# Last inverses of the first attention repeated on TensorE instead of through device memory, one-product gate bias, and a norm that lags two tiles

## The reference

```
xn = layernorm(x)
# layer 0, attention: 16 heads, two softmax maps per head, 32 output columns per head
a1, a2 = softmax(q1 k1' / 4 + causal), softmax(q2 k2' / 4 + causal)
lam    = exp(sum(lambda_q1*lambda_k1)) - exp(sum(lambda_q2*lambda_k2)) + 0.2
out    = (a1 - lam * a2) @ v                       # [T, 512]
out    = groupnorm over (time, 32 columns) of each head, times gn_w plus gn_b
s      = (0.8 * out) @ Wo
# layer 0, gate
g      = silu(mxfp4(xn) @ mxfp4(weight).T + bias)
x      = x + s * g
xn     = layernorm(x)                              # input of layer 1: attention and experts
```

## Time and profile before

| | |
|---|---|
| median of 3 runs | 843.96 us (841.63, 843.96, 844.77) |
| profiled execution | 842.62 us, of which the span of the trace is 840.9 us |
| PE busy | 775.1 us, 92% of the span |
| DVE / ACT / POOL busy | 530.1 / 429.3 / 425.7 us |
| granted TensorE clock, slices of 21 us | full, except 0.5 in the slice 378 to 399 us and 0.8 in the one after |
| middle block | 375.5 to 466.6 us |

### The profile page before, as it was taken

How to read it: one execution, slowest core, us unless ns; L and a number is a source line. 1 busy time by engine, 2 the same in 40 slices (tenths; PEclk the granted TensorE clock), 3 DMA queues, 4 the chain that set the end, 5 groups by cost and what they waited for, 6 DMA issues and landing times. The chain is left out here.

```text
span 840.9 us, 13145 instructions
## 1 busy us (share of the span) xinstructions
PE 775.1 (92%) x3822; PEld 376.3 (45%) x3826; DVE 530.1 (63%) x1352; ACT 429.3 (51%) x922; POOL 425.7 (51%) x754
## 2 busy tenths in 40 slices
PE   2988999999999999985889899999889999999995
PEld 2353222222222222221655323333167888888883
DVE  3657887778777777603562688787066654555556
ACT  2431466666666666661223157777744454455552
POOL 1661465664224324422232122334378997799994
PEclk9999999999999999995899999999999999999997
DMA  6391751020011002012019445235332221112221
GB/s 188 115 291 65 177 117 30 20 61 15 21 41 39 21 18 63 15 39 82 0 67 240 149 108 140 92 108 181 97 106 66 67 62 60 49 64 62 62 66 57
DMA packets 57960, 69.84 MB, mean 83 GB/s; under 512 B 13813, under 2 KB 35670, under 8 KB 57895
## 3 DMA queue, kind: packets, MB, share of 16 engines
q1 hardware_dynamic: 57820, 69.08, 29.2%
q10 hardware_dynamic: 80, 0.07, 0.0%
HBM read 47.35 MB, written 15.47 MB: 75 GB/s over the span
## 5 line engine op out<-in xcount | busy, mean ns | idle before, releaser
L763 ACT ACTIVATE top<-ps 128x512 f32<-128x512 f32 (+3 forms) x384 | 170.6, 491 | 132.5 <-PE ps L691 132.5
L691 PE MATMUL ps<-mid 99*128 99x512 bf16 (+3 forms) x576 | 182.5, 332 | 4.2 <-ACT mid L763 3.1
L808 DVE CUSTOM_DVE_ANT_0 ps<-ps,keep 128x512 f32<-128x512 f32 (+3 forms) x320 | 161.8, 530 | 30.3 <-PE ps L667 30.2
L667 PE MATMUL ps<-mid 96*128 96x512 bf16 (+3 forms) x512 | 167.1, 339 | 4.6 <-DVE mid L808 1.0
L711 PE MATMUL ps<-top,mid 128*33 128x512 f32 (+3 forms) x768 | 161.7, 500 | 0.0
L1559 PE MATMUL ps<-xp,wp 128*128 128x512 f32 (+1 forms) x600 | 146.8, 394 | 5.4 <-ACT wp L1609 3.6
L691 PEld LDWEIGHTS ps<-mid 99*128 99x128 bf16 x576 | 53.5, 97 | 173.0 <-ACT top L763 103.3
L1559 PEld LDWEIGHTS ps<-xp,wp 128*128 128x128 f32 (+1 forms) x600 | 112.4, 188 | 31.9 <-ACT xp L1611 4.1
L900 POOL TENSOR_SCALAR_AFFINE_SELECT top<-top 128x128 f32<-128x128 f32 x256 | 71.2, 292 | 106.1 <-ACT top L763 104.1
L763 ACT ACTIVATE mid<-ps 128x512 f32<-128x512 f32 (+1 forms) x192 | 82.1, 494 | 63.3 <-PE ps L691 40.6
L812 DVE TENSOR_REDUCE top<-ps 128x1 f32<-128x512 f32 x128 | 88.3, 690 | 33.0 <-PE ps L667 32.8
(11 more groups left out here) (208 smaller groups left out, 887.0 us busy)
## 6 DMA issues: line engine op xcount, KB each, us to landing
mid<-part_scratch SPq DMA_DIRECT2D x9, 1152.0 KB, 8.8
part_scratch<-top SPq DMA_DIRECT2D x18, 384.0 KB, 5.1
top<-in_w SPq DMA_DIRECT2D x12, 528.0 KB, 4.7
cw_s<-combine_rows SPq DMA_DIRECT2D x48, 128.0 KB, 3.0
part_scratch<-top SPq DMA_DIRECT2D x18, 256.0 KB, 5.1
mid<-part_scratch SPq DMA_DIRECT2D x9, 384.0 KB, 4.2
top<-inverse_scratch SPq DMA_DIRECT2D x12, 256.0 KB
top<-in_w SPq DMA_DIRECT2D x6, 512.0 KB, 6.5
```

Of the source, the lines that this page charges most:

```text
L667: nc.tensor.matmul(ps[:, s_bank(turn), 0:w], queries(pair, m)[0:PARTS, i * P:(i + 1) * P], keys(pair, m)[0:PARTS, c * 512:c * 512 + w], st ...
L691: nc.tensor.matmul(ps[:, ST_BANK + n % AHEAD, 0:w], keys(pair, m)[0:STACK, j * P:(j + 1) * P], queries(pair, m)[0:STACK, q0:q0 + w], start ...
L763: nc.scalar.activation(pr[:, n % RING, 0:w], ps[:, ST_BANK + n % AHEAD, 0:w], ACT.Exp, scale=0.25).then_inc(p_ready, 1)
L808: ins = nc.vector.tensor_tensor_reduce(bank, bank, msk[:, 512 - w:512], -1.0 if low else 1.0, 3e38 if low else -3e38, ALU.add, ALU.min if ...
```

## The change

In words, in the order of the program:

- **Bias.** The bias is loaded on 65 partitions (it was one). DVE splits it in three bf16 parts on all of them and puts them in the rows 0, 32 and 64 of a `bip` of 65 rows that is zero elsewhere. `row` has 65 rows of ones. `ffn(t)` then has one bias product in place of three.
- **Last inverses.** For the last heads of the first attention alone, `inverses` is replaced by `inverse_rows`: one DMA from `cd[:, c, 0, :]` (128x32) to eight rows of 512 in SBUF, `repeated(c)[0][0:8, :]`. PE repeats them (`repeat_rows`): two fp32 products of 8x128 against 8x512, with a 0/1 matrix `heads` that POOL writes at the start of the block from the identity. c = 0 goes to the banks 6 and 7 ahead of all else on PE; c = 1 to the banks 2 and 3 behind ffn(1). ffn(4) waits until c = 0 has been read (`row_stats` 7).
- **Division.** `divide` on DVE does what POOL's `scale` and DVE's `combine` did: map 1 times lambda times its bank, map 0 times its bank, the sum, and `bn_stats`. It stands first on DVE for c = 0, and behind gate2(1) for c = 1. POOL has no division left in the middle block. gate2(2) and gate2(3) move behind the scaling. SP no longer waits for the inverses before it loads the next weights.
- **Norm two behind.** DVE does `norm2(t-2)` in tile t, PE the transposes of t-3 and the logits of t-4, and the first two projections one step later in the loop, which has one turn more.

```diff
-        bip = sb("bip", [1, 3, D], BF16, keep)
+        bip = sb("bip", [65, D], BF16, keep)
...
-                    sp.dma_start(bia[:, :], fb).then_inc(ld_r, 16)
+                    sp.dma_start(bia[:, :], fb.partition_broadcast(65)).then_inc(ld_r, 16)
...
-                    link(nc.vector.tensor_copy(bip[:, 0, :], bia[:, :]))
-                    link(nc.vector.tensor_tensor(bir[:, :], bia[:, :], bip[:, 0, :], ALU.subtract))
-                    link(nc.vector.tensor_copy(bip[:, 1, :], bir[:, :]))
-                    link(nc.vector.tensor_tensor(bip[:, 2, :], bir[:, :], bip[:, 1, :], ALU.subtract))
+                    link(nc.vector.memset(bip[:, :], 0.0))
+                    link(nc.vector.tensor_copy(bih[:, :], bia[:, :]))
+                    nc.vector.tensor_copy(bip[0:1, :], bih[0:1, :])
+                    link(nc.vector.tensor_tensor(bir[:, :], bia[:, :], bih[:, :], ALU.subtract))
+                    link(nc.vector.tensor_copy(bim[:, :], bir[:, :]))
+                    nc.vector.tensor_copy(bip[32:33, :], bim[32:33, :])
+                    link(nc.vector.tensor_tensor(bip[64:65, :], bir[64:65, :], bim[64:65, :], ALU.subtract))
...
+            def inverse_rows(sp, c):
+
+                sp.wait_ge(inv, 2 * LASTF + c + 1)
+                sp.wait_ge(scaled, 2 * (LASTF - 1) + c + 1)
+                sp.dma_start(repeated(c)[0][0:8, :], cd[:, c, 0, :]).then_inc(inv_r[c], 16)
+
+            def repeat_rows(pe, c, heads, banks):
+
+                pe.wait_ge(inv_r[c], READS * LASTF + 16)
+                for m, bank in enumerate(banks):
+                    last = nc.tensor.matmul(ps[:, bank, :], heads[:, m, :], repeated(c)[0][0:8, :], start=True, stop=True)
+                return last
+
+            def divide(dve, c, banks):
+
+                to, n1 = o1[:, LASTF, columns(c)], second(LASTF)[:, c, :]
+                nc.vector.scalar_tensor_tensor(n1, n1, lamv[:, 1:2], ps[:, banks[1], :], ALU.mult, ALU.mult).then_inc(scaled, 1)
+                dve.wait_ge(scaled, 2 * LASTF + c + 1)
+                nc.vector.tensor_tensor(to, to, ps[:, banks[0], :], ALU.mult).then_inc(combined, 1)
+                dve.wait_ge(combined, 2 * (LASTF + c) + 1)
+                nc.vector.tensor_tensor(to, to, n1, ALU.add).then_inc(combined, 1)
+                dve.wait_ge(combined, 2 * (LASTF + c) + 2)
+                nc.vector.bn_stats(st6o[:, LASTF, c, :], to).then_inc(row_stats, 1)
...
-                env["last_inverses0"](sp)
+                env["inverse_rows"](sp, 1)
...
+                for m in range(2):
+                    nc.gpsimd.tensor_copy(heads[:, m, :].rearrange("p (h d) -> p h d", h=4),
+                                          idf[0:8, m:8:2].unsqueeze(2).to_broadcast([8, 4, 32])).then_inc(bip_ok, 1)
                 nc.gpsimd.memset(row[:, :], 1.0).then_inc(bip_ok, 1)
-                env["last_scaled0"](pool)
...
+                dve.wait_ge(tot, 1)
+                env["divide"](dve, 0, (6, 7))
                 env["last_inverted0"](dve)
...
-                env["last_combined0"](dve, 0)
-                for t in range(4):
+                for t in range(2):
                     gate2(t)
-                link(env["last_scaled_odd0"](dve))
-                env["last_combined0"](dve, 1)
+                dve.wait_ge(tot, 2)
+                env["divide"](dve, 1, (2, 3))
...
-                    if t >= 1:
-                        norm2(dve, t - 1)
+                    if t >= 2:
+                        norm2(dve, t - 2)
...
+                pe.wait_ge(bip_ok, 3)
+                env["repeat_rows"](pe, 0, heads, (6, 7)).then_inc(tot, 1)
...
-                    for j in range(3):
-                        last = nc.tensor.matmul(z, row[:, :], bip[:, j, :], start=False, stop=j == 2)
-                    last.then_inc(f_mm, 1)
+                    nc.tensor.matmul(z, row[:, :], bip[:, :], start=False, stop=True).then_inc(f_mm, 1)
...
                 for t in range(NT):
+                    if t == 4:
+                        pe.wait_ge(row_stats, 7)
                     ffn(t)
+                    if t == 1:
+                        env["repeat_rows"](pe, 1, heads, (2, 3)).then_inc(tot, 1)
                     if t >= 6:
                         total(t - 6)
```

More of the change, by code:

```diff
@@ L225, in program @@
             le = sb("le", [P, 2], F32)
-            bia, bir = (sb(n, [1, D], F32) for n in ("bia", "bir"))
+            bia, bir = (sb(n, [65, D], F32) for n in ("bia", "bir"))
+            bih, bim = (sb(n, [65, D], BF16, keep) for n in ("bih", "bim"))
             ld_x, ld_w, ld_c, ld_f, ld_r = (sem(n, a) for n in ("ld_x", "ld_w", "ld_c", "ld_f", "ld_r"))
@@ L524, in last_inverses @@
                 inverses(sp, LASTF, 1)
[L525 to L526 removed]
+            def inverse_rows(sp, c):
[16 more added lines that the diff above has]
+                nc.vector.bn_stats(st6o[:, LASTF, c, :], to).then_inc(row_stats, 1)
             def last_inverted(dve):
                 inverted(dve, LASTF, 1)
[L531 to L532 removed]
             def last_scaled(eng):
                 scale(eng, LASTF, 0)
[L536 to L541 removed]
+                scale(eng, LASTF, 1)
             with ExitStack() as b:
@@ L978, in _ @@
                             sp.dma_start(w2s[0:NI - (GI - 1) * P, GI - 1, :], w2[(GI - 1) * P:NI, :]).then_inc(ld_m, 16)
-                        inverses(sp, LASTF, 0)
+                        if first:
+                            inverse_rows(sp, 0)
+                        else:
+                            inverses(sp, LASTF, 0)
                         sp.wait_ge(landed, 32 * (N + 1))
             here[1] = kept
-            return o1, combined, last_inverses, last_inverted, last_scaled, last_combined, last_outputs, last_scaled_odd
+            if first:
+                return last_outputs, last_inverted, inverse_rows, repeat_rows, divide
+            return o1, combined, last_outputs, last_inverted, last_inverses, last_scaled
         tmp[1] = 0
@@ L1002, in late0 @@
                 far_maps0(sp, pair + 1)
-        o0, combined0, last_inverses0, last_inverted0, last_scaled0, last_combined0, last_outputs0, last_scaled_odd0 = attention(
+        last_outputs0, last_inverted0, inverse_rows, repeat_rows, divide = attention(
             0, stack0, v0, 16, loaded0, late0)
@@ L1040, in late1 @@
                 far_maps1(sp, (3, 1)[pair])
-        o1, combined1, last_inverses, last_inverted, last_scaled, _, last_outputs, _ = attention(
+        o1, combined1, last_outputs, last_inverted, last_inverses, last_scaled = attention(
             1, stack1, v1, 8, loaded1, late1)
@@ L1072, in middle @@
         bip = env["bip"]
-        row = sb("row", [1, P], BF16)
+        row = sb("row", [65, P], BF16)
+        heads = sb("heads", [8, 2, P], F32)
         aT = sb("aT", [P, KD, T], BF16, mid)
@@ L1246, in _ @@
                                                 ALU.mult, ALU.add).then_inc(yd_ok, 1)
-                for t in range(4, NT):
+                for t in range(2, NT):
                     gate2(t)
@@ L1324, in _ @@
                 pe.wait_ge(q_ev, 3)
-                pe.wait_ge(bip_ok, 1)
                 def ffn(t):
@@ L1369, in project @@
                     last.then_inc(proj, 1)
-                for t in range(NT + 3):
+                for t in range(NT + 4):
                     if t < NT:
@@ L1391, in _ @@
                         last.then_inc(x_tr, 1)
-                    if t == 2:
+                    if t == 3:
                         pe.wait_ge(ldw, 64)
-                    if t >= 3:
-                        logits(t - 3)
-                    if t == 7:
+                    if t >= 4:
+                        logits(t - 4)
+                    if t == 8:
                         project(0)
```

23 lines of the change are left out of this document (7 added, 16 removed).

## The result

The changed kernel takes 831.48 us, the median of five executions (829.60 to 834.52), against 844.17 for the kernel before: a ratio of 0.9862, 95% interval 0.9843 to 0.9880. That is 11.7 us less (10.1 to 13.3 by the interval). Measured once more beside other runs of before, it took 830.32, ratio 0.9852 [0.9830, 0.9875]. The forecast was 834.2, 9.0 us less than the 843.2 that it started from.

What follows compares the result with a forecast made beforehand. PE is nearly full except at the middle block's start, bound by the transfer chain to c = 1's statistics, then the norm loop. Gains 6.7 + 0.3 + 2.0 = 9.0 us from 843.2 give 834.2 us, range 830.0 to 839.0.

Steps and rivals of the forecast that it cites:

- Inverses: Middle block: last group statistics of c = 1 end at 389.4 us against 396.13, a gain of 6.7 us.
- Second total: Middle block, PE: the wait for ffn(7) between the two totals shrinks with three products instead of five, 0.3 us.
- Bias "worth nothing more": Middle block gate: beyond 0.3 us the bias products bring nothing, as the gate had finished eight us early.
- Norm loop: From output product to logits: DVE's wait for POOL goes, PE limits at 2.65 us a tile against 2.94; gain 2.0 us.
- First gate product: Middle block, PE: delayed by the repeat products from 379.53 to 381.1 us, covered by the gate's slack.
- First block: Bias split on 65 partitions: three more DVE instructions, some 2 us covered by 6 us; cost 0, at worst 0.5.
- Behind the logits: Projections, splits and scratch writes follow the logits one for one; the block ends near 457.5 us.
- 1 (the clock holds through c = 1's products): Middle block: c = 0's repeats shorten PE's pause, so c = 1's run at full clock; 1.6 us more, 832.6 us; chance 0.22.
- Rival 2: Middle block: PE's full clock returns before the output product, the stretch being denser in rows; about 830 us; chance 0.10.
- rival 3: Small gain: ACT's piece slow (1.2), POOL's copies 2 us (1.0), loop stays at 2.94 (1.2); 837 us; chance 0.14.
- Rival 4: End of block: the DMA queue's writes set the end, half or more of the gain waited out; 839 to 843 us; chance 0.06.
- Rival 5: Slower: the direct copy into eight partitions crawls, gain gone at 10.4 us, 847 us if it takes 14; chance 0.03.

Runs made afterwards that it cites:

- after_again: The changed kernel with no edit, measured again on the chip of later runs: 830.32 us, ratio 0.9852 to the kernel before.
- before_bias: The kernel before with the one-product bias alone: 840.80 us, ratio 0.9977 to the kernel before.
- after_bias3: The changed kernel with the bias again as three one-row products and the four-instruction split: 835.76 us, ratio 0.9917 to the kernel before.
- after_scratch: The kernel before with the one-product bias and the norm two behind, inverses still through device memory: 836.52 us, ratio 0.9923 to the kernel before.
- early_wide_fill2: early_wide plus sixteen unread PE products ahead of the output product and six ahead of the third projection: 825.56 us, ratio 0.9792 to the kernel before.
- early_wide: The changed kernel with c = 1's reciprocal first on DVE, its repeat and division ahead of the gate, and 128-row repeat products: 826.17 us, ratio 0.9791 to before.
- early: The changed kernel with c = 1's reciprocal first on DVE, its repeat ahead of ffn(0), its division ahead of all gate2: 827.36 us, ratio 0.9817 to before.
- after_lag1: The changed kernel with the norm again one tile behind: 835.56 us, ratio 0.9920 to the kernel before.
- fill: The changed kernel with eight unread 128x512 bf16 products behind the second total, ahead of the output product: 831.90 us, ratio 0.9859 to the kernel before.

## Why the prediction was right, and where it was not

Forecast, and what the changed kernel and its repetition show, as gains over before at each landmark of the block (from the table):

| gain at | forecast | changed | after_again |
|---|---|---|---|
| first `total` | 6.7 | 5.0 | 4.5 |
| output product | 7.0 | 5.3 | 4.8 |
| last logits | 9.0 | 9.6 | 7.9 |
| end of the block | 9.0 | 10.3 | 9.6 |

The forecast of 834.2 us was near 831.5, and the order of the chain came as drawn up. That the gain at the end of the block was near too was in part luck: one term was too high and another too low.

- **Inverses, 6.7 forecast, 4.5 to 5.0 measured: the mechanism right, the term too large.** POOL's start took 0.7 us as said (375.12 to 375.83). The first repeat took 2.75 us where 1.9 at full clock was said: the clock fell at 376.9, inside it. `divide` took 2.92 (387.77 to 390.69), as said 3.0. The reciprocal started at 381.46, forecast 381.4, released by DVE, with ACT's piece long landed. The copy took 2.14 us from issue to PE (381.82 to 383.96), where I took 1.4 from the write to device memory in the earlier trace rows. Two things were wrong with that row: over all twelve of its kind in the trace of before (line L474) such writes landed in 1.4 to 2.0 us, median 1.7, so I had taken the quickest; and SP spends 0.70 us on issuing the direct copy, 0.33 on that write. DMA: Bandwidth & Descriptors in the Trainium skill, section Anatomy of one DMA, has about 2.0 of fixed cost, fitted to transfers that GpSimd issues; this one is SP's, and its 2.14 agrees with the page better than with the row that I let decide. The second repeat took 3.78, forecast 3.5, at the half clock that was forecast. That is 0.9, 0.7 and 0.3 us too little.
- **Second total, 0.3:** 1.43 us behind the first, before 1.72. Right.
- **Bias "worth nothing more": wrong as a statement on the change, harmless in the sum.** In before_bias it holds in the main. But the edit is what lets five gate tiles pass between the second repeat and the first `total`; after_bias3 shows the `total` 2.6 to 3.1 us late without it. I had counted the shorter tiles (as 0.8 us each, they take 0.64) and given the whole to the inverses.
- **Norm loop, 2.0 forecast, 4.3 and 3.1 measured: PE's floor was mis-sized.** The limit did pass from DVE's wait to PE, as said, but a tile is 2.39 us and not 2.65. I had added 0.88 us from 418.79 to 419.67 for transposes and logits, which held gaps that belonged to PE's own wait; in the changed kernel they take 0.58 (410.34 to 410.92), and the eight products 1.81 to the first transpose. Of the 2.3 us between forecast and measurement the last four tiles bring 1.1 (406.22 to 415.71 is 9.5 us, where I had 10.6), the first four 0.6 (to 406.22, 9.0 for 9.6), and what follows the last tile 0.6 (6.3 for 6.9). In after_again the clock came back later, 6.0 us behind the output product's start for 3.6 here (before 4.6), which makes the loop 1.2 us longer there.
- **First gate product** at 382.06, forecast 381.1, with no consequence. **First block:** its cost does not show. The middle block starts at 375.17 and 374.51 in the two traces of the changed kernel and at 375.53 before; a cost of 0.5 us could not be told from that spread.
- **Behind the logits** the moves were to go on one for one. They did, and 0.6 us (after_again 1.6) more came until the end of the block, at 455.98 where 457.5 was forecast. In the changed kernel SP's last twelve writes start 9.7 us earlier in the block than before, as the logits do, and take 13.3 us for 13.9: the 0.6 lie in that queue. after_again has the clock at full behind the logits, where before (434.8 to 438.2) and the changed kernel (424.7 to 428.1) have a stretch at half; its twelve writes start 1.4 us further ahead than its logits. That the clock is the reason was not tested.
- **The rest:** the block gives 10.3 and 9.6 in the profiled executions, the medians 11.7 and 12.2. The mean granted clock of the whole program is between 0.963 and 0.977 in every execution of the two kernels. What lies between is of the size of the half-clock stretches that come and go in the other stages; no run settles it.

Of the **rivals**, 1 (the clock holds through c = 1's products) did not happen: half from 376.9 to 400.8. (Before, the clock fell at 380.2, not 380.4 as I read it, which changes nothing in the sum.) The kernels with 128-row repeats are those in which the second repeat ran at full clock. Rival 2 (clock back before the output product) did not either: without the one-row products the clock still came back only in the output product, though its guess that rows matter was the right one. The gate alone decides nothing: with one bias product and no repeats the clock was back at 385.3, inside the gate, in after_scratch, and stayed at half throughout in before_bias. None of rival 3's three losses came: ACT's piece landed in 2.3 us, POOL's writes took 0.7, the tiles are 2.39. Rival 4 took nothing from this change, as the block's end moved by more than the logits; it does take most of what early_wide_fill2 adds on PE. Rival 5 needed 10.4 us for the copy, which took 2.14.

**A version that beats both:** early_wide, 826.17 us, ratio 0.9791 [0.9765, 0.9817] to the kernel before; the fillers add nothing that can be measured.

## What to carry to other kernels

- Price a step at the clock it will run at, and ask what stands ahead of the engine behind it: taking a product away is worth nothing while the engine waits afterwards (before_bias, 12.43 us idle) and its full length when it is queued ahead of the chain (after_bias3). Single contributions then need not add up.
- Read an engine's floor from a stretch in which it never waits. Rows with small waits between them overstate it, and the gain is understated.
- A selection product with a few rows can be given 128 rows for the price of writing zeros (0.35 us here), if the chain runs behind it at half clock; unread products hold a full clock across a pause but are of little use once it is down. Before adding either, see where the next queue is full.

## What I had not expected of the hardware

- **Rows bring the clock back.** Eight-row fp32 products at half clock, PE busy in each us, left it at 0.50; with 128 rows and the same columns it was back at 379.5, and in none of the seven kernels with eight rows before 388. Each is one trace, and other things count too, as after_scratch and before_bias show.
- **16 KB from SBUF to SBUF in pieces of 128 bytes takes 2.14 us** from issue to the waiting engine (2.18 in early), where the same bytes to device memory landed in 1.4, and in up to 2.0 elsewhere in that trace. Issuing alone took 0.70 and 0.33 us.
- **The moment the clock falls varies by execution of the same work.** The first eight-row repeat took 1.98 us at full clock in early, after_lag1 and fill, 2.75 in the changed kernel and 3.21 in its repetition; the clock fell between 375.8 and 378.6.
